# Four graph layers on one core: unread products on the matmul engine in the waits after the last recurrent step

## The reference

```python
def reference(x, adj, nodemask, ...):
    h = relu(layernorm(x))
    for l in range(5):                        # layer 1: gated recurrent unit, 5 layers
        agg = (adj != 0)^T @ (h @ weight[l])
        gi, gh = agg @ w_ih.T + b_ih, h @ w_hh.T + b_hh
        r, z = sigmoid(gi_r + gh_r), sigmoid(gi_z + gh_z)
        h = (1 - z) * tanh(gi_n + r * gh_n) + z * h
    x = x + h * nodemask

    h = relu(layernorm(x))                    # layer 2: gated mix of two products
    n = (sum|adj| + 1e-6) ** -0.5
    hom = n * (adj @ (n * (h @ theta)))
    gate = sigmoid(h @ W_t + b_t)
    x = x + elu(gate * hom + (1 - gate) * (h @ W_h))

    h = relu(layernorm(x))                    # layer 3: two convolutions on 5 groups of the first 25 nodes
    for g, idx in enumerate(GROUPS):
        A = normalised(adj[idx, idx] + I)
        t = relu(A @ (h[idx] @ W1[g]) + b1[g])
        fused[idx] += softmax(fusion_w)[g] * relu(A @ (t @ W2[g]) + b2[g])
    x = x + fused

    h = relu(layernorm(x))                    # layer 4: one convolution on the whole graph
    return x + relu(nodemask * (normalised(adj + I) @ (h @ W.T + b)))
```

## Time and profile before

| | before |
|---|---|
| time, median of 3 runs | 786.41 us (785.37 to 789.0) |
| time of the profiled execution | 786.07 us |
| its span from first to last instruction | 784.3 us |
| mean granted TensorE clock | 0.956 |
| PE busy | 695.3 us (89%), 4091 products |
| DVE busy | 600.0 us (77%) |
| ACT busy | 522.0 us (67%) |
| POOL busy | 298.9 us (38%) |

### The profile page before, as it was taken

One profiled execution on the slowest core, in us unless ns is written; L12 is line 12 of the kernel. 1 busy time (PEld: TensorE's weight loads), 2 busy tenths in 40 slices (PEclk: granted clock), 3 DMA queues, 4 the chain that ended last, 5 costly groups with the idle time before them and its releaser, 6 DMA issues.

```text
span 784.3 us, 12362 instructions
## 1 busy us (share of the span) xinstructions
PE 695.3 (89%) x4091; PEld 586.6 (75%) x4091; DVE 600.0 (77%) x1461; ACT 522.0 (67%) x1083; POOL 298.9 (38%) x423
## 2 busy tenths in 40 slices
PE   3899799999999988989999989989999989966865
PEld 3777588788878777878878777878878767765644
DVE  4698997888978966988978966988976967865143
ACT  5566577577778767578768767578776567565433
POOL 4212524553344245363344244373322245342220
PEclk9899999999999999999999999999999999978569
DMA  6610021000000012200000020200000000200001
GB/s 152 163 30 1 2 56 43 14 1 6 5 1 1 27 31 68 81 15 3 10 1 1 7 51 28 61 21 4 9 1 1 1 1 28 67 15 10 2 1 55
DMA packets 47624, 21.08 MB, mean 27 GB/s; under 512 B 9033, under 2 KB 47561, under 8 KB 47561
## 3 DMA queue, kind: packets, MB, share of 16 engines
q1 hardware_dynamic: 47560, 20.29, 9.5%
HBM read 15.27 MB, written 4.19 MB: 25 GB/s over the span
## 4 chain that ended last, share of the span: by engine, by line
PE 42%; DVE 31%; ACT 12%; POOL 9%; issue 5%; DMA 1%; DVEq 0%; SPq 0%; POOLq 0%; ACTq 0%
PE bank L405 6%; PE bank L406 6%; PE bank L407 6%; PE bank L400 5%; DVE zd L1314 4%; DVE hd L1326 4%; DVE h L1318 4%; DVE rh L1337 3%; DVE bank L1340 3%; POOL rstd L925 3%; ACT bank L897 2%; ACT xn L700 2%; PE bank L535 2%; PE bank L600 2%; POOL h_lo L941 2%
## 5 line engine op out<-in xcount | busy, mean ns | idle before, releaser
L941 POOL TENSOR_TENSOR h_lo<-h,h_hi 128x512 fp32r<-128x512 f32 x64 | 81.9, 1280 | 334.0 <-DVE h_hi L1321 334.0
L405 PE MATMUL bank<-h_hi,whh_hi 128*128 128x512 f32 x240 | 107.8, 449 | 13.3 <-DVE rh L1337 12.7
L1337 DVE SCALAR_TENSOR_TENSOR rh<-bank,rh 128x512 f32<-128x512 f32 x80 | 54.9, 687 | 66.8 <-ACT bank L891 66.8
L405 PE MATMUL bank<-g_hi,wc_hi 128*128 128x512 f32 x240 | 103.5, 431 | 0.7 <-DVE h L1318 0.3
L407 PE MATMUL bank<-h_lo,whh_hi 128*128 128x512 f32 x240 | 97.2, 405 | 0.0
L406 PE MATMUL bank<-h_hi,whh_lo 128*128 128x512 f32 x240 | 96.9, 404 | 0.0
L407 PE MATMUL bank<-g_lo,wc_hi 128*128 128x512 f32 x240 | 94.8, 395 | 0.0
L406 PE MATMUL bank<-g_hi,wc_lo 128*128 128x512 f32 x240 | 94.8, 395 | 0.0
L400 PEld LDWEIGHTS bank<-edge,hn 128*128 128x128 f32 x640 | 84.5, 193 | 9.8 <-DVE edge L1040 2.6
L700 ACT ACTIVATE xn<-x_res,shift,rstd 128x128 f32<-128x128 f32 x128 | 55.8, 485 | 49.4 <-POOL shift L927 49.3
L400 PE MATMUL bank<-edge,hn 128*128 128x128 f32 x640 | 85.2, 276 | 2.2 <-DVE edge L1040 2.2
(11 more groups left out here) (167 smaller groups left out, 1645.0 us busy)
## 6 DMA issues: line engine op xcount, KB each, us to landing
x_in<-in_x SPq DMA_DIRECT2D x8, 512.0 KB, 5.4
adj_in<-in_adj SPq DMA_DIRECT2D x8, 512.0 KB, 4.8
x_res<-in_x SPq DMA_DIRECT2D x16, 256.0 KB, 2.8
out_x<-x_res SPq DMA_DIRECT2D x16, 256.0 KB, 2.3
xz<-x_res SPq DMA_DIRECT2D x16, 50.0 KB
w_sb<-in_L_gnn_W SPq DMA_DIRECT2D x1, 640.0 KB, 5.2
w_sb<-in_L_gnn_W SPq DMA_DIRECT2D x5, 128.0 KB, 5.2
rows<-in_adj SPq DMA_DIRECT2D x32, 0.6 KB
```

The costliest lines, as they stand in the source:

```text
L405: nc.tensor.matmul(dst[:], w_hi, m_hi, start=start, stop=False)
L941: nc.gpsimd.tensor_tensor(h_lo[q][:], h[q][:], h_hi[q][:].bitcast(f32), ALU.subtract).then_inc(sem["h_lo_new"], 1)
L1337: nc.vector.scalar_tensor_tensor(rh[:], R_BANK[:], 1.0, rh[:], ALU.add, ALU.mult).then_inc(sem["rh_ready"], 1)
```

## The change

A new helper `keep_busy(r, products)` issues, in the last round only, so many products of 128 x 512 of the first recurrent weight with the first quad's state into bank `TG`. No semaphore is set by them and nothing reads their result. The helper is called at the head of seven functions, ahead of the function's first wait.

```diff
+            def keep_busy(r, products):
+
+                if r == ROUNDS - 1:
+                    for _ in range(products):
+                        nc.tensor.matmul(TG[:], whh_hi[:, 0, :], h_hi[0][:], start=True, stop=True)
...
             def turn_and_sum(r, q):
 
                 u = r * QUADS + q
+                keep_busy(r, (14, 0, 8, 5)[q])
                 pe.wait_ge(sem["ln1_xn"], u + 1)
...
             def turn_zone(r, q):
+                keep_busy(r, (5, 12, 3, 3)[q])
                 pe.wait_ge(sem["ln2_xn"], r * QUADS + q + 1)
...
             def l2_support2(r, k):
                 g, b0, G, n = TILES[k]
+                keep_busy(r, 2)
                 pe.wait_ge(sem["l2_hid_read"], r * NT + k + 1)
...
             def turn_back(r, q):
+                keep_busy(r, (5, 3, 4, 0)[q])
...
             def turn_last_norm(r, q):
                 u = r * QUADS + q
+                keep_busy(r, 7 if q == 0 else 0)
                 pe.wait_ge(sem["ln3_xn"], u + 1)
...
             def l3_linear(r, q):
+                keep_busy(r, 2)
                 pe.wait_ge(sem["ln3_h"], r * QUADS + q + 1)
...
             def l3_aggregate(r, q):
                 u = r * QUADS + q
+                keep_busy(r, 3)
                 pe.wait_ge(sem["adjTI_scaled"], u + 1)
```

## The result

The changed kernel takes 775.68 us (median of 4 runs, 774.86 to 776.93). The kernel before took 786.92 us beside it (4 runs). The ratio is 0.986, 95% interval 0.9835 to 0.9886. The prediction was 774.9 us, between 772.0 and 780.0. The profiled execution took 774.86 us, with a span of 773.1 us; before, 784.3.

What follows compares the result with a forecast made beforehand. The prediction took TensorE's halved clock behind the last step as the bound. Layer 2's 3.2, layer 3's 5.9 and layer 4's 2.1 us sum to 11.2, from 786.07 to 774.9 us, range 772.0 to 780.0.

Steps and rivals of the forecast that it cites:

- What bounds it: Behind the last step TensorE's clock is halved in stretches, and the rest waits for it: 19.57 us busy of 23.80.
- The price of an unread product: 0.24 us at full clock, 0.43 at half; nothing where PE waits for an engine that gets no faster, otherwise in full.
- Layer 2: Quads 0 and 2 at full clock: a gain of 3.2 us, bounds 1.6 and 4.0.
- The part that quad 0 gives on: In layer 2, of the 2.38 us quad 0 saves, 1.6 reaches quad 1's gate and all behind it.
- The bound by POOL and the unbroken DVE work: In layer 2, quad 1's `xn` waits for POOL, and 4.7 us of DVE work before its gate is unbroken.
- Layer 3: From the second zone turn on, full clock gains 3.5 + 3.0 - 0.6 = 5.9 us.
- the products on the path: Unread products in layer 3 that PE's waits don't hide; the gain is 5.9 us, 7.4 if all were hidden.
- Layer 4: Turns back and first quad at full clock: a gain of 2.1 us, bounds 1.5 and 2.5.
- The second fall: Rival: the clock falls again at the turn back, layer 4's gain is lost; gain 6.5 us, 779.6 us; chance 0.19.
- That the change does nothing: Rival: behind the last step a faster PE finds ACT and DVE late; 783 to 786 us; chance 0.09.
- the clock falls where it fell: Rival: 0.50 through 722 to 745 and unread products cost 0.43 each; 7.7 us more, 793.8 us; chance 0.06.
- The risk that the prediction took from that sentence: Between the last conv and layer 4's first product, 4.5 us of products alone would have to hold the clock.

Runs made afterwards that it cites:

- e1: Changed kernel with all 107 unread products kept in place but 32 columns wide instead of 512: 787.85 us, ratio 1.0021 to the kernel before.
- e2: Changed kernel with six of the seven calls removed, leaving only the 27 unread products of layer 2's turns: 782.98 us, ratio 0.9958 to the kernel before.
- e11: Repeat of e3, the changed kernel without the 18 unread products ahead of layer 3's second support products: 774.2 us, ratio 0.9842 to the kernel before.
- e10: Changed kernel with unread products ahead of layer 3's second support products only where PE waits, none ahead of layer 4's first aggregate: 773.97 us, ratio 0.9854.
- e5: Changed kernel without the 39 unread products of the turns back and of layer 4: 775.76 us, ratio 0.9873 to the kernel before.
- e4: Changed kernel with each unread product replaced by two unread transposes of 128 x 128: 773.63 us, ratio 0.9842 to the kernel before.
- e6: Changed kernel with unread products only in the long waits, none ahead of layer 3's second support products, other turns or layer 4's products: 775.29 us, ratio 0.9858.
- e3: Changed kernel without the 18 unread products ahead of layer 3's second support products: 772.55 us, ratio 0.9834 to the kernel before.
- e12: e10 plus 18 unread products of 128 x 384 in one wait within the steps, at about 94 us: 773.16 us, ratio 0.983 to the kernel before.
- e9: Changed kernel without the 12 unread products ahead of the second zone turn: 776.81 us, ratio 0.9887 to the kernel before.

## Why the prediction was right

- **What bounds it** was right. e1 shows that it is the clock, held by work, and e2 that the gain of a stretch is its own. In reading the page's line the text left out a slice: the last five read 7, 8, 5, 6 and 9, and the 7 holds the start of layer 2.
- **The price of an unread product** was right: 0.24 us at full clock in the chain. In the long waits the products cost nothing, since PE still waited for ScalarE behind them.
- **Layer 2**: 3.2 us forecast, 3.20 measured. Quads 0 and 2 took 3.41 each, as quad 3 had the earlier trace rows. The part that quad 0 gives on was right too: quad 2's first turn came 1.35 us earlier than 704.25, which with the later start of 0.25 is the 1.6 of the text; quad 3's came 3.2 earlier in the same way. The bound by POOL and the unbroken DVE work is what made 3.2 of 4.0: the difference at 695.08 is the text's 694.8 with the later start.
- **Layer 3**: 7.62 us were forecast between the second and the fourth zone turn and 7.75 measured (719.84 to 727.59); 10.0 from there to k6, and 10.08 measured (727.59 to 737.67); 0.6 lost behind it, and 0.4 measured (6.36 us before, 6.77 after). Together 5.9 and 5.88. That the sum fits to 0.02 is in part luck, since two gains came out 0.1 smaller and the loss 0.2 smaller. For the products on the path the text had about 1.5 us, and e11 measures 1.25; it was right to give k1's nothing, though the chain names them. (The terms written for the second zone add up to 4.06 to 4.16, not 4.18.)
- **Layer 4**: 2.1 forecast, 2.37 measured. To the first bias product it was 0.87 for 0.90. The first quad took 4.55 us (752.12 to 756.67) for 4.80: the three products ahead of the first aggregate cost 0.13 instead of 0.37, and e10, without them, has the 4.42 of the later quads. The later quads stayed 4.42 apart. The three stretches gave 0.25 more than the 11.2 forecast, nearly all of it here, and the steps ended 0.25 later. That the profiled execution meets 774.9 to 0.04 is luck.
- **The rivals.** The second fall did not come, but e5 shows that its mechanism is real: without the products at the turns back the clock falls there and 1.76 us are lost. That the change does nothing, or that the clock falls where it fell, was wrong; e1 is what that looks like (787.85 us, not the 793.8 worked out with 0.43 us for each product; its narrow ones cost 2.2 us more in layer 3 and nothing more in layer 4).
- **The Trainium skill** (TensorE: Matmul & The Clock Gate, Part 4: PE-mode transpose) has it that transposes don't count as a busy TensorE. e4 says otherwise for this kernel's transposes: 214 of them in the place of the 107 products held 1.00 to the end. The risk that the prediction took from that sentence was not there. In e5, where the turns stand alone with waits between them, the clock fell.

What stays open is why the clock is lost for 20 us in one kernel of thin work (e6) and for one piece or not at all in another (e3, e11). The same kernel differed between executions (e3 and e11), so something that varies from one to the next has a part in it; the counts that are safe were not found out.

## What to carry to other kernels

Where the granted clock dips late in a kernel, see which engine ends last inside the dip: unread products are worth their place where TensorE does (layer 3, 24.82 us busy of 30.48) and nothing where another engine covers the loss (5.03 us with the clock and without). A gain on TensorE counts only if the engine that takes its result is early too: e12's 1.5 us were gone at the next state (9.82 us for 9.83). Fill the long waits by their length at the full-clock price, leave out the places where TensorE has no wait unless the clock is lost without them, and judge it by the stretch in the profile and by the spread of several executions, since one of them can keep a clock that the next one loses.

## What was not expected of the hardware

- Transposes of 128 x 128 held the clock as products did (1.00 through 24.45 and 21.01 us).
- A clock lost at the start of layer 3 stayed lost for about 20 us with PE busy 25.32 of 29.65 us (e6), and came back within 7 us where unread products stood ahead of each tile and turn (e9), within 4 us without those ahead of the tiles (e3).
- A product of 32 columns takes about 0.12 us (14 in 1.72), half of what one of 512 columns takes at full clock, and did not hold the clock (0.59 in layer 3).
